# A four-stage attention chain on one core: the order in which the engines take the steps of their lanes

## The reference, cut to what matters

```
L0: x = x + MHA8(LN(x), LN(ctx))              # 8 heads of 32
    U = (LN(x) @ W_in.T + b_in) @ Bmat        # 64 states
    s_t = silu(s_{t-1} @ A.T) + U_t           # a scan over the 1024 rows
    x = x + s @ Cmat + mean(probs) @ W_prog.T + b_prog
L1: x = x + attention(LN(x), LN(ctx)), 16 heads of 64, causal mask
L2: x = LN(x + attention(x, ctx)), 16 heads of 16, mask, denominator + 1e-9
L3: x = x + attention(LN(x), LN(ctx)), 16 heads of 16, mask per batch
    x = x + gelu(LN(x) @ fc1 + b1) @ fc2 + b2  # 1024 hidden
```

## Time and profile before

| | us |
|---|---|
| median of 3 runs | 1373.41 |
| lowest and highest | 1372.36, 1373.49 |
| the profiled execution | 1372.36 |
| its span | 1370.6 |
| PE busy in it | 1330.6 |
| DVE, ACT, POOL busy | 904.9, 673.8, 557.2 |

### The profile page before, as it was taken

How to read it: one execution, slowest core, us unless ns; L and a number is a source line. 1 busy time by engine, 2 the same in 40 slices (tenths; PEclk the granted TensorE clock), 3 DMA queues, 4 the chain that set the end, 5 groups by cost and what they waited for, 6 DMA issues and landing times.

```text
span 1370.6 us, 22991 instructions
## 1 busy us (share of the span) xinstructions
PE 1330.6 (97%) x8763; PEld 1123.3 (82%) x8763; DVE 904.9 (66%) x2204; ACT 673.8 (49%) x1495; POOL 557.2 (41%) x700
## 2 busy tenths in 40 slices
PE   6999999999999999999999999999999999899999
PEld 5889987787888788878888888779877987688778
DVE  4778872777656766676577566773768467746771
ACT  4667766134554444544445534445344543464453
POOL 4464431107513652364245311572166216621661
PEclk9999999999999999999999999999999999999999
DMA  6154402200000000000000001000000000000000
GB/s 150 36 116 132 132 20 81 65 8 1 1 17 17 1 12 6 17 0 9 1 9 1 25 5 29 0 1 17 16 1 1 20 12 1 1 5 12 1 1 17
DMA packets 48363, 34.10 MB, mean 25 GB/s; under 512 B 22077, under 2 KB 45436, under 8 KB 48252
## 3 DMA queue, kind: packets, MB, share of 16 engines
q1 hardware_dynamic: 46919, 32.44, 8.6%
q10 hardware_dynamic: 1332, 0.17, 0.1%
HBM read 23.26 MB, written 8.39 MB: 23 GB/s over the span
## 4 chain that ended last, share of the span: by engine, by line
PE 86%; DVE 6%; POOL 4%; ACT 2%; issue 1%; DMA 0%; ACTq 0%; SPq 0%; DVEq 0%
PE ps L886 11%; PE ps L876 10%; PE ps L836 10%; PE ps L932 8%; PE ps L855 8%; PE ps L943 8%; PE ps L846 6%; PE ps L896 6%; PE ps L802 5%; PE ps L785 5%; PE ps L1037 2%; PE ps L1050 1%; DVE mx L1351 1%; POOL pr L1607 1%; POOL pr L1621 1%
## 5 line engine op out<-in xcount | busy, mean ns | idle before, releaser
L1582 POOL TENSOR_TENSOR rstd<-mv,halfneg 128x1 f32<-128x1 f32 x192 | 108.1, 565 | 339.1 <-DVE mv L1317 337.5
L1621 POOL TENSOR_TENSOR pr<-mx,pr 128x616 f32<-128x616 f32 x128 | 155.8, 1219 | 216.7 <-DVE mx L1351 215.4
L1163 ACT ACTIVATE pr<-pr 128x616 f32<-128x616 f32 x224 | 159.8, 716 | 148.6 <-POOL pr L1621 78.3
L1167 ACT ACTIVATE pr<-ps 128x512 f32<-128x512 f32 x224 | 132.8, 595 | 161.8 <-PE ps L855 161.6
L886 PEld LDWEIGHTS ps<-vtab,pr 128*128 128x128 f32 (+1 forms) x1280 | 153.3, 192 | 14.6 <-ACT pr L1167 10.1
L886 PE MATMUL ps<-vtab,pr 128*128 128x102 f32 (+1 forms) x1280 | 161.9, 275 | 2.3 <-ACT pr L1167 0.9
L855 PE MATMUL ps<-ident,pr 128*128 128x128 f32 (+1 forms) x1120 | 160.0, 276 | 3.7 <-POOL pr L1607 2.9
L1142 ACT ACTIVATE tt<-ps 128x256 f32<-128x256 f32 x160 | 61.0, 382 | 182.3 <-PE ps L785 182.0
L855 PEld LDWEIGHTS ps<-ident,pr 128*128 128x128 f32 (+1 forms) x1120 | 125.9, 140 | 29.9 <-POOL pr L1607 9.4
L876 PE MATMUL ps<-vwo,pr 128*128 128x256 f32 (+1 forms) x640 | 148.9, 381 | 0.0
L836 PE MATMUL ps<-wk,tt 128*128 128x308 f32 x512 | 144.9, 424 | 0.0
(11 more groups left out here) (200 smaller groups left out, 2364.4 us busy)
## 6 DMA issues: line engine op xcount, KB each, us to landing
out_dram<-xt SPq DMA_DIRECT2D x64, 128.0 KB, 1.7
xt<-in_x_dram SPq DMA_DIRECT2D x32, 128.0 KB, 2.2
xt<-out_dram SPq DMA_DIRECT2D x32, 128.0 KB, 2.0
fc<-in_L_xattn_fc_w_dram SPq DMA_DIRECT2D x2, 1024.0 KB, 6.4
wk<-in_L_xattn_wkv_dram SPq DMA_DIRECT2D x4, 512.0 KB, 4.7
front<-in_L_xattn_wkv_dram SPq DMA_DIRECT2D x4, 512.0 KB, 5.8
wo<-in_L_xattn_wo_dram SPq DMA_DIRECT2D x1, 1024.0 KB, 7.8
kb<-in_L_xattn_wq_dram SPq DMA_DIRECT2D x1, 1024.0 KB, 5.5
```

What stands on the lines that cost most here:

```text
L1163: ac(v, v, ACT.Exp, scale=-ATTN[key[0]].scale).then_inc(done["expo"], 1)
L1167: ac(pr[:, run.lane, 0:4 * P], bank(run.lane, 0), ACT.Copy).then_inc(done["pturn_main"], 1)
L1621: p.tensor_tensor(p8, mx[:, run.lane, :].unsqueeze(2).to_broadcast([P, HG, KEYS]), p8, ALU.subtract).then_inc(done["below"], 1)
```

## The change

Only the five strings of `TURNS` change. The plans, the steps, their instructions, waits and operands are the same; each engine takes the same steps, lane by lane in the same order within a plan, but interleaves the plans in another way. Compared by place in the engine's list, 548 of 1522 steps of PE stand elsewhere (by 10 places at most), 809 of 2165 of DVE (13), 317 of 1027 of ACT (6), 192 of 649 of POOL (7) and 52 of 175 of SP (6). The moved steps lie mostly in the set-up and phase 1 (up to 200 us of the trace before), and then around 262 to 325, 475, 590 to 640, 670 to 750, 905 to 960, 1040 to 1110, 1180 to 1270 and after 1320 us. Cut to the strings that hold the first steps:

```diff
 TURNS = {
     "tensor": (
-        "iiiiii0i0i1iii1iii2i102iii2i0i1i0ii10ii01ii130231030210130132132032101032201323012310031012012310230323021032012"
...
+        "iiiiiii1i0iii10iii2i10ii21ii0ii0i1ii2i01ii0310230310210231031213023022013010233102031301201132102102302103202303"
...
     "scalar": (
-        "iiiii0iii1021ii2i0i10i1ii201ii3032100301311203101203221230331002012311030123021302220100323312011123031032123220"
...
+        "iiiiiii0i1021i1ii0i0i21ii0ii123032103003121103021013220231303020123101103210213022023010323321030121130131202322"
...
     "gpsimd": (
-        "i012ii2i303i1011001122033203201310011223302003a0121311a222032303030111122223003003311112202030233113012221302033"
...
+        "ii102i2i3i130010001112232302303001111220202303a31301a12012020320331311122220303031013121220230303101312212203303"
```

More of the change, by code:

```diff
@@ L241 @@
[L241 to L250, removed]
@@ new lines @@
+        "0210213310321321023101210320310312230102320310321321102312120320213023230130013210210313120203210312320320120301"
+        "3032102313210213021321023132032013310321302102310321123013123203231023130121323021323012a3a23aasaaaasaasasasasas"
+        "asasasaasaasaasaasaasaasaasaasasaasasasaasasasaasaasasaasaasasaaaaasaaaaasaaa0aa23s01011232030102121320303010120"
+        "1212312020310313123020201011313230202012131030302321201010230232103101201020130231320110132132130103012210210323"
+        "0120131012130330210313201020303132102013202123030310312120210130102323201200101032130321302110131132013120231013"
@@ new lines @@
+        "2103202102103120312321032202310332332313032120203103123120120232310313130202012313010320210212131030020321320110"
+        "1021031213230103031231212032030120130132212312203013202331301230302012313112030210212132030130313210202013031312"
+        "0120203210303132b1b212313bbbbbb32bb2bb23bb3bbb2b32bbbbbb32bbbbbbbb23bbbbb3bbbbb2bbbbbbb202b030132213012030323123"
+        "0103102320231031232102123120303131321020200313131210202032330131120202131312302020130132031210020003123130211310"
+        "1223231022120323130123130230201301301321212032023103131230202010131313202020123131303002121230130302012132103103"
@@ new lines @@
+        "1200210302102312310312221301223230201331313023202031030123210212132030313131202020301313112020202313103130202121"
+        "0310320301212130130320120003101212031213213223210230323301213012303021023131032120120320313231301020202313131012"
+        "020232331310120202313130120203213101321020312030303213123321232321"),
+    "vector": (
+        "i0ii11023120ii2i3iii001131000i01i110ii22001012100113322122320033323223012100300310301130011021211313102022203212"
+        "1020002323020331003303113113221110203132210223000220211330002103302333131111322111012033222230222121200330033310"
+        "0030332023111112111212002230322200230233031301030303031232111120021211331220123220200323033031313030231211011021"
+        "3322111322102032333220233311330012211330200113102123322323323sssssssssssssssssssasasasasassasasasaasaaasaaasasaa"
+        "aaaaasaassaaasaa0a00a0a11121323302023010012101231021223233013200300110212301123123233312002110322000310011112133"
+        "0222000221000111030101313301233221211002223210123233002003331320231310031210002202123311111212030203300332222001"
+        "3110113030011011100301300331022211110122110021212023233000331001213312301103003232000203122003023113133200311121"
+        "2301110003032112220221001131102030332220332212211222300133311100033332332300101010110323112211102312001032030101"
+        "3121210312221230033110333320002222003133223322211013213123030302320102022032110103032311133131121230011303200222"
+        "0103221133301013023222100110230222122321311330303202030332311010112200030232110311133102033100202110321212102331"
+        "1333003110220200220021223212131333011200033230303010232110102230211112311312303031312203001001132310122200223100"
+        "033311023312211212223233322023333333221323bb22bb232bb3323322bbbbbbbbb3b22232bb3bbbbbbbbbbbbbbb0000333b3010110100"
+        "2010121220201100301223032132320121331213331232010222312332333031102020300111133210122200022003010333110103302111"
+        "2221030121233231203223323110033023120111213032200212300003311232311121300202203032131330301011002222201111102222"
+        "1233000130230311101213330331223122230032333231010302023100111121330222000212000111303330101102133212211002322233"
+        "3110232330023001333112201100323012002110322111331233030220002223231030131110003302222211101211002302301302332110"
+        "2113132303313222320202133230331130202030101113312102220002230001303311130030121112221100213222333022121303033001"
+        "3323112011002330100221102321113132332200030022223013101113030330102222211013103012020301232320112110133231332232"
+        "1322003233230311000300312211130311000222200020321330301110331121222103012123323123223302311003330012211303121002"
+        "2321233110003023121121333333232220231"),
@@ L290 @@
     "sync": (
-        "01230123aaaaaa0a1a0a12aa23a0a3a01a1aaaaa2203031aa1aa2a23300a1a12aa2aa30aa03a1a1a2aa2303011223301200a01312213323b"
-        "bbbaa00112233001122330123000111bb223332001122330011223302130213"),
+        "01230123aaaaaaa001aa1a23aa02aaaa0a3a11a203203a1a1aaa202a303a1a1a2a2a0a3a0a3a1a1a2a2a030311223031200a01312213323b"
+        "bbbaa00112233001122330123000111bb223332001122330011223302130231"),
 }
```

49 lines of the change are left out of this document (14 added, 35 removed).

## The result

The changed kernel is slower: 1383.94 us median of 6 runs (1378.32 to 1384.23) against 1373.45 for the kernel before in the same sessions, a ratio of 1.0072 with a 95% interval of 1.0052 to 1.0090. Its times fall into two groups: 1378.32 and 1378.41, and then 1383.78 to 1384.23 four times. The profiled execution took 1379.43 us, so it belongs to the lower group. The granted clock of the upper group is 0.994 on the mean, that of the lower one 0.998 to 0.999. The later sessions repeated the changed kernel; of all 23 recorded executions seven took 1378.21 to 1379.43 us and sixteen 1383.78 to 1385.47, so the upper group is the usual one.

The account below looks back on a forecast made before the run. The prediction took TensorE (PE), busy 1330.6 of 1370.6 us, as the bound, leaving at most 40.0 us of idle time. Its terms summed to 2.8 us gained, 1373.4 to 1370.6 us, range 1366.5 to 1376.5.

Parts of the forecast that it names:

- Start, +0.8: 10 to 43 us: ACT's copies of `v0_lay` start earlier behind `value_zero`, shifting PE's work forward; 0.8 us gained.
- Masks, −1.0: 82 to 92 us: rstd behind POOL's masks delays the norm, PE waits about 2.5 us; 1.0 us lost.
- Scan's end, −0.3: 262 to 275 us: `gap_turn` and `ends` come later, so `ssm.s@0:8` begins at 267.3; 0.3 us lost.
- Norm places: 591 to 598, 1041 to 1050, 1185 to 1188 us: norms no longer stretched beside `below`; 0.8, 0.7, 0.5 us gained.
- 904 us, +0.4: PE's 0.82 us wait for lane 3's heads: earlier `pturn.3.0@0:12` and its exponential fill about half a later wait; 0.4 us gained.
- the rest, +0.9: All other changed places: small waits go about as often as they come, with a small surplus; 0.9 us gained.
- Function tables, 0: ACT, about 935 us: one more pair of table loads, 2.6 us of ACT, hidden behind PE; costs nothing.
- Rival 2: Start: PE idle at 12 to 13.5 brings another low-clock stretch, 1.75 us lost, giving 1372.3 us; chance 0.08.
- Rival 3: DVE and POOL: new meetings of norm and POOL, up to 1.04 us each; six give 1376.8 us; chance 0.18.
- three quarters of 0.42: Share of the forecast case (chance 0.42, range 1368.5 to 1372.5 us) under 1370.66; entered as 0.33 for faster.
- "same": Whole kernel: no change beyond the about 0.2% that a measurement can tell; chance given as 0.37.

Follow-up runs that it names:

- experiment 9: Kernel before with the new order only before 22, at 22 to 59, 22 to 41.6 or 41.6 to 59 us: medians 1374.14, 1374.20, 1380.03, 1375.37 us.
- Experiment 7: Kernel before with POOL's masks step moved from 82 to about 214 us: 1373.45 us; the same plus the new order of 59 to 200 us: 1373.71.
- experiment 3: Kernel before with the new order only for the steps of 200 to 300 us: 1376.32 us, ratio 1.0024.
- experiment 6: Kernel before with the new order on PE and DVE only for 255 to 269.6 us (last scan steps, verdict): 1375.20 us, ratio 1.0015.
- experiment 5: Kernel before with the new order only for 586 to 602, 1036 to 1056 and 1176 to 1193 us: 1371.54 us, ratio 0.9989.
- experiment 4: Kernel before with the new order only for the steps from 300 us on: 1374.80 us, ratio 1.0007.
- experiment 8: Changed kernel with 12 unused matmuls put into PE's wait at 26.3 to 29.6 us: 1378.70 to 1379.20 us and 1384.78, 1384.80.
- experiment 11: Kernel before with the new order at the three norm places and the masks moved into the scan: 1370.58 us, ratio 0.9983.
- experiment 1: Kernel before with the new order only for steps begun before 59 us: 1375.11 to 1375.73 and 1381.07 to 1382.48 us, ratio 1.0033.

## Why the prediction was wrong, step by step

I forecast 1370.6 us, within 1366.5 to 1376.5, with 0.20 for slower. Measured: 1383.94. The sum was wrong in these steps:

- **Start, +0.8: no gain, a loss.** The step "these begin when `value_zero` is done" was the failure. The copies need two releases, which lay 0.04 us apart in the trace (POOL's last copy ended at 22.14, DVE's item 14 at 22.18), and I followed only one: in the new order `value_zero` is done first and the values of items 11 to 14 decide. Nor did `value_zero` come 0.8 us earlier; it ended at 22.45. With that, "PE stands still longer at 12 to 13.5, which costs nothing as long as the query work fits later" fell too, as the place where it went is in front of item 11. By the means of experiment 9 the steps before 22 us lose about 1.1 us. The 0.8 net of the changed kernel is one pair of traces, and the profile before has one of the earliest starts of all, so its size is not shown.
- **Masks, −1.0: right mechanism, wrong size.** The wait was found with its cause (forecast about 2.5 us, measured 1.98). The low clock behind it was missing, and the rest of phase 1's order, to which I gave nothing. Changed kernel: 2.7, of which 1.7 is the low clock. Experiment 7: with the masks in the scan the low clock behind them is gone and phase 1 costs nothing.
- **Scan's end, −0.3: wrong size by ten.** I saw the `ssm` at 267.3 and took PE as covered by table steps. I left out that the `ssm` waits for ACT's branch on a value from DVE, so that each step put in front of `gap_turn` or `agree` delays all four lanes at once, and that the last scan step moves too. Changed kernel: 3.1; 2.9 us alone (experiment 3), 2.4 of them from the last scan steps and the verdict (experiment 6).
- **Norm places, +0.8 +0.7 +0.5 = +2.0: right.** 0.49 + 0.60 + 0.93 = 2.03 alone (experiment 5), each single one off by up to 0.4.
- **904 us, +0.4, and the rest, +0.9: wrong.** 904 gave nothing (0.1 at most, the wrong way); the rest from 300 us on lost 2.5 us (experiment 4). I had called the rest the weakest term, and took a surplus without having followed it.
- **Function tables, 0: right.**
- **Rival 2, the clock at the start, 0.08: the right kind, far too small.** I priced one more stretch of 3.5 us at half clock. The second low clock, 10.2 us within 35 to 49, costs some 5 us, and comes in most runs: four of the six, sixteen of all 23. It decides the median. It did not follow from idle time at 12 to 13.5, where I looked for it (experiment 9, new order before 22 us: one group), and it does not need the wait at 26 to 29.6 (experiment 8). Without the upper group the kernel would have been at 1378.4, 5.0 us slower, and outside my range still.
- **Rival 3, slower by new meetings of norm and POOL, 0.18:** not this. There are four long norms, before there were six.

In sum, 0.8 + 2.7 + 3.1 + 0.3 = 6.9 us of the two profiles' 7.1 are waits and the clock behind them. The profile before is 1.05 us under its median and the one after about 1 us above the lowest of its group, so between the usual runs of before and the lower group it is some 5 us; the other 5.5 of the medians' 10.5 are, by the mean clocks, the second low clock.

Two slips of arithmetic in the prediction changed nothing: three quarters of 0.42 are 0.32 and not 0.33, and the chance of "same" would be 0.38.

**Open.** What in the steps of 22 to 41.6 us sets off the low clock at 36 to 50 us in a part of the runs is not settled. Shown is that these steps suffice, that the steps before 22 and behind 41.6 us didn't do it in ten runs each, and, by one profile, that PE need not have been idle in the 14 us ahead. It also stays open why the same order has the low clock at the start for 0, 3.4 or 6.8 us from one execution to the next. The order there puts the eight 64-row score matmuls of lane 2 behind the mixes and fills 38 to 50 without a gap; neither was tried by itself.

## What to carry to other kernels

An order moved near a point on which all lanes depend (a branch on a computed value, a long step on a helper engine, a chain of set-up items) has to be followed through every step up to that point: the local waits that it fills are worth tenths, the point is worth microseconds. Where two releases lie close together in the trace, work out both, because the change may move only one. A gain in a reordering shows up in the places where it can be followed; a term for "the rest" should be zero with a wide range. A wait of 2 us can bring a low clock of 3.4 us behind it, which nearly doubles its price (1.98 + 1.7 us here). And before a difference of 1 us near the start of a trace is read, traces of kernels with the same start should be compared with each other.

## What the runs showed of the hardware that was not expected

- PE's granted clock fell to 0.50 behind the wait of 1.98 us at the masks in all four profiles that have it (low at 91.2 to 94.6 in the changed kernel), and behind the wait of 2.8 to 3.6 us at the start in 15 of 16; the sixteenth, of experiment 11, had waited 2.76 us. It did not fall there when PE was kept busy (experiment 8). Behind a wait of 1.76 us near 1170 to 1184 us, which all 17 profiles have, it fell in five; behind the 1.36 us near 90 us of the old order in none of ten. The Trainium skill, "TensorE: Matmul & The Clock Gate", section "Part 1: The HAM clock gate (the "warmup" mystery)", has the clock gated by how busy PE has been; that the first fall is gone in experiment 8 agrees with that, that its second one came behind 14 us of busy PE does not.
- With the new order at 22 to 41.6 us a second low clock, 10.2 us long within 35 to 49 us, goes with the upper group of times: 3 of 6 runs in experiment 1, 4 of 10 and 8 of 10 in experiment 9, 16 of 23 of the changed kernel. No run without these steps is in such a group. PE was busy all the while it lasted, and in experiment 8 for 14 us ahead of it. The kernel's time then has two values 5 to 6 us apart.
- The low clock comes at other places in single runs too (598 to 601 us in experiment 7, 1178 to 1185 in experiments 1 and 3 and two of experiment 9, 1171 to 1175 in experiment 11, 3.4 us long and 1.6 us lost each). It is likely the main part of the 1.5 to 3 us by which the times of one kernel spread, since the higher times have the lower mean clocks.
- Whether a VectorE norm over 128x256 is stretched by a GpSimd step over 128x616 (L1621 or L1607) hangs on less than 0.1 us. In the traces of before, after and experiment 5 it took 1.31 to 1.47 us each time that step began from 0.18 us ahead of it to 0.09 us behind its start, and 0.40 to 0.42 us each time the step began 0.13 us or more behind its start.
